# Macaron layer on one core: rope on even and odd tiles, one normalising op, and half of the output projection in the next sample's first slot

## What is computed

```
qkv = layernorm(x) @ Wqkv.T                      # 16 heads of 16 features
q = cos * q + rotate_half(q) * sin               # rotate_half: (x0, x1) -> (-x1, x0)
k = cos * k + rotate_half(k) * sin
scores = where(causal, q @ k.T / 4, -inf)
out = softmax(scores) @ v
x = x + out @ Wo.T
```

## Time and profile before

| | |
|---|---|
| median of 3 runs | 2371.58 us (2366.81 to 2373.09) |
| the profiled execution | 2371.06 us, its span 2369.3 us |
| instructions | 53760 |
| busy, share of the span | PE 90%, DVE 82%, ACT 57%, POOL 54% |
| granted TensorE clock, mean | 0.981 of full |
| attention stage, steady | 680 to 1840 us of the span, clock 1.00 |
| one steady sample | 45.57 us |

### The profile page before, as it was taken

The page is one execution under the profiler, slowest core; times in us unless marked ns, Lnnn a source line. Parts: engine busy times, 40 slices in busy tenths (PEclk is TensorE's granted clock), DMA queues, the critical chain, the costliest instruction groups (busy, mean ns, idle before and its releaser), DMA issues. The chain is left out here.

```text
span 2369.3 us, 53760 instructions
## 1 busy us (share of the span) xinstructions
PE 2140.1 (90%) x18188; PEld 1161.5 (49%) x18188; DVE 1946.5 (82%) x4345; ACT 1358.6 (57%) x2567; POOL 1283.0 (54%) x1459
## 2 busy tenths in 40 slices
PE   2999999489999999999999999999999986999999
PEld 1666666324444444444444444444444433666666
DVE  4777777469999999998999899899899865777776
ACT  2555545136666676666666666666666663455444
POOL 3666666335545554554555455455455425666664
PEclk9999999779999999999999999999999997999999
DMA  4566666333454444444445444444444513666664
GB/s 157 179 201 202 202 207 198 94 63 88 93 97 90 91 101 98 91 95 86 91 98 100 91 90 98 89 100 95 89 90 97 93 37 126 201 203 199 201 201 165
DMA packets 280353, 295.33 MB, mean 125 GB/s; under 512 B 45744, under 2 KB 263184, under 8 KB 280080
## 3 DMA queue, kind: packets, MB, share of 16 engines
q1 hardware_dynamic: 279536, 290.85, 48.8%
q10 hardware_dynamic: 544, 1.05, 0.1%
HBM read 140.08 MB, written 83.89 MB: 95 GB/s over the span
## 5 line engine op out<-in xcount | busy, mean ns | idle before, releaser
L820 ACT ACTIVATE at_probs<-at_st_ps 128x512 f32<-128x512 f32 x1280 | 748.2, 604 | 473.7 <-PE at_st_ps L925 466.8
L753 DVE TENSOR_REDUCE at_mx<-at_mx_ps 128x1 f32<-128x512 f32 (+3 forms) x1408 | 837.7, 633 | 125.9 <-PE at_mx_ps L907 124.7
L675 POOL TENSOR_SCALAR_AFFINE_SELECT at_probs<-at_probs 128x512 f32<-128x512 f32 x512 | 319.1, 635 | 677.9 <-ACT at_probs L820 673.9
L925 PE MATMUL at_st_ps<-at_q_stack,at_k_stack 49*128 49x512 f16 (+3 forms) x2048 | 459.8, 302 | 73.2 <-ACT at_probs L820 71.0
L902 PE MATMUL at_mx_ps<-at_k_stack,at_q_stack 48*128 48x512 f16 (+3 forms) x2048 | 494.1, 304 | 29.8 <-DVE at_mx L753 18.5
L431 ACT ACTIVATE f_h<-f_h_ps,f_b1s 128x512 f32<-128x512 f32 x256 | 175.9, 687 | 358.3 <-PE f_h_ps L473 347.2
L925 PEld LDWEIGHTS at_st_ps<-at_q_stack,at_k_stack 49*128 49x128 f16 x2048 | 135.9, 94 | 460.4 <-ACT at_probs L820 339.8
L907 PE MATMUL at_mx_ps<-mask,turn 64*128 64x128 bf16 (+2 forms) x1408 | 342.6, 244 | 0.0
L942 PE MATMUL at_pv_ps<-at_probs,at_v 128*32 128x512 f32 (+3 forms) x4096 | 329.8, 440 | 0.8 <-POOL at_probs L675 0.6
L489 PE MATMUL f_y_ps<-f_w2hi,f_hlo 128*128 128x256 f16 x1024 | 279.2, 273 | 0.0
L489 PE MATMUL f_y_ps<-f_w2lo,f_hhi 128*128 128x256 f16 x1024 | 279.2, 273 | 0.0
(11 more groups left out here) (117 smaller groups left out, 3921.9 us busy)
## 6 DMA issues: line engine op xcount, KB each, us to landing
at_q_stack<-qk_image SPq DMA_DIRECT2D x192, 128.0 KB, 4.5
at_k_stack<-qk_image SPq DMA_DIRECT2D x192, 128.0 KB, 4.8
f_x<-in_x SPq DMA_DIRECT2D x32, 512.0 KB, 5.6
f_w1hi<-w_hi SPq DMA_DIRECT2D x128, 128.0 KB, 2.4
f_w1lo<-w_lo SPq DMA_DIRECT2D x128, 128.0 KB, 2.1
f_b2s<-in_b SPq DMA_DIRECT2D x128, 128.0 KB, 3.8
f_w2hi<-w_hi SPq DMA_DIRECT2D x128, 128.0 KB, 4.2
f_w2lo<-w_lo SPq DMA_DIRECT2D x128, 128.0 KB, 4.3
```

Source lines behind the costliest of these rows:

```text
L675: nc.gpsimd.affine_select(out=ap, in_=ap, compare_op=ALU.is_ge, fill=0.0, base=0, pattern=[[0, d] for d in dims] + [[1, P]], channel_multi ...
L753: nc.vector.tensor_reduce(o_ap, i_ap, AX_X, ALU.max).then_inc(max_done, 1)
L820: nc.scalar.activation(probs[:, c, :], st_ps[c % 2][:], ACT.Exp, scale=DH ** -0.5).then_inc(exp_done, 1)
L925: ins = nc.tensor.matmul(bank[:, col:col + T - q0], k_stack[ss.par][rows, j + ha, kt * P:(kt + 1) * P], q_stack[ss.par][rows, j + ha, q0:T ...
```

## The change

1. **Rope.** The host permutes the columns of Wqkv for Q and K, so that a pair of tiles (t = 0 and 1 of Q, 2 and 3 of K) holds the even features of all heads and the odd ones. Rope is then even * cos - odd * sin and odd * cos + even * sin, between two tiles, without a swap of partitions. DVE only multiplies by the cosines. ACT gets a new op, `rope_raw`, which copies the projected tile from PSUM to the SBUF tile `raw` for POOL, once DVE's product is done. POOL makes the two products with the sines first (`rope_sin`), then the two sums (`rope_sums`), after the masks of the slot.
2. **Halves later.** In slots 1 and 2, ACT's high halves go from steps 0 and 2 to 3 and 5, DVE's low halves from steps 0 and 3 to 4 and 7. The products with the cosines stand at steps 3 and 6 of slot 0 and 2 and 6 of slot 1, the copies at steps 4 and 7 and 3 and 7.
3. **One normalising op.** The four multiplications of 4 x 16 columns become one of 4 x 4 x 16.
4. **Output projection.** Its tiles 2 and 3 move from step 10 of slot 3 to step 0 of the next sample's slot 0. `project_qk`'s first tile there moves to steps 1 and 2, and the second residual to step 2.
5. The rows of the DRAM image are read back with another pattern, to match the new order of features. Number and size of the DMAs stay.

```diff
@@ -526,7 +526,7 @@
...
         xT = Split(sb("xThi", [P, NC, T], F16), sb("xTlo", [P, NC, T], F16))
-        swapped = [sb(f"swapped{i}", [P, T], F32) for i in range(2)]
+        raw = [sb(f"raw{i}", [P, T], F32) for i in range(2)]
         by_cos = [sb(f"by_cos{i}", [P, T], F32) for i in range(2)]
@@ -555,6 +555,7 @@
...
         xT_lo, qk_done, rope_in, sin_done = sem("xT_lo"), sem("qk_done"), sem("rope_in"), sem("sin_done")
+        cos_done = sem("cos_done")
         rope_done, qk_hi, qk_lo, v_done = sem("rope_done"), sem("qk_hi"), sem("qk_lo"), sem("v_done")
@@ -604,7 +605,7 @@
...
                     for at, lo in enumerate(rows):
-                        img = image[2 * part + lo].rearrange("(j a r) n -> a r j n", a=2, r=DH)[par]
+                        img = image[2 * part + lo].rearrange("(r j a) n -> a r j n", a=2, r=DH)[par]
                         sp.dma_start(stack[HP * par + DH * at:HP * par + DH * at + DH, :, :], img).then_inc(
@@ -675,14 +676,19 @@
...
 
-            def rope(n, t):
+            def rope_sin(n, t):
                 idx = 4 * n.b + t
                 pool.wait_ge(rope_in, idx + 1)
-                nc.gpsimd.tensor_tensor(by_sin[t % 2][:], swapped[t % 2][:], sin_t[:], ALU.mult).then_inc(sin_done, 1)
-
-                wait(pool, qk_lo, idx - 1)
-                pool.wait_ge(sin_done, idx + 1)
-                nc.gpsimd.tensor_tensor(rotated[t % 2][:], by_cos[t % 2][:], by_sin[t % 2][:], ALU.add).then_inc(rope_done, 1)
+
+                wait(pool, rope_done, 4 * n.b + t // 2 * 2)
+                nc.gpsimd.tensor_tensor(by_sin[t % 2][:], raw[t % 2][:], sin_t[:], ALU.mult).then_inc(sin_done, 1)
+
+            def rope_sums(n, u):
+                pool.wait_ge(sin_done, 4 * n.b + 2 * u + 2)
+                for e, op in ((0, ALU.subtract), (1, ALU.add)):
+
+                    wait(pool, qk_lo, 4 * n.b + 2 * u - 1 + e)
+                    nc.gpsimd.tensor_tensor(rotated[e][:], by_cos[e][:], by_sin[1 - e][:], op).then_inc(rope_done, 1)
 
@@ -692,7 +698,8 @@
...
                 if g < 2 and sample(s + 1):
-                    rope(s + 1, 2 * g)
+                    rope_sin(s + 1, 2 * g)
+                    rope_sin(s + 1, 2 * g + 1)
                 if g == 2 and sample(s + 2):
@@ -711,7 +718,7 @@
...
                 if g < 2 and sample(s + 1):
-                    rope(s + 1, 2 * g + 1)
+                    rope_sums(s + 1, g)
             schedule(pool, slot)
@@ -724,8 +731,7 @@
...
                 wait(dve, rope_done, idx - 1)
-                nc.vector.tensor_tensor(by_cos[t % 2][:], x_ps[t % 2][:], cos_t[:], ALU.mult)
-                nc.vector.stream_shuffle(swapped[t % 2][:], x_ps[t % 2][:], [i ^ 1 for i in range(32)]).then_inc(rope_in, 1)
+                nc.vector.tensor_tensor(by_cos[t % 2][:], x_ps[t % 2][:], cos_t[:], ALU.mult).then_inc(cos_done, 1)
 
@@ -766,12 +772,10 @@
...
                 dve.wait_ge(inverse_done, G - 2)
-                for i in range(NT):
-                    ins = nc.vector.tensor_tensor(
-                        on[os.par][:, i, :].rearrange("p (j q d) -> p j q d", q=2, d=DH)[:, j:j + GH, half, :],
-                        turned[:, i, :, 0:DH],
-                        inverse[:, GH * i:GH * i + GH].rearrange("p (a d) -> p a d", d=1).broadcast_to([P, GH, DH]), ALU.mult)
-                ins.then_inc(on_done, 1)
+                nc.vector.tensor_tensor(
+                    on[os.par][:].rearrange("p i (j q d) -> p i j q d", q=2, d=DH)[:, :, j:j + GH, half, :],
+                    turned[:, :, :, 0:DH],
+                    inverse[:].rearrange("p (i a d) -> p i a d", i=NT, d=1).broadcast_to([P, NT, GH, DH]), ALU.mult).then_inc(on_done, 1)
 
@@ -782,11 +786,11 @@
...
                         maxima(s, g, n)
-                    if g in (1, 2) and sample(s + 1) and n in (0, 3):
-                        rope_low(s + 1, 2 * (g - 1) + (n == 3))
+                    if g in (1, 2) and sample(s + 1) and n in (4, 7):
+                        rope_low(s + 1, 2 * (g - 1) + (n == 7))
                     if group(G - 3) and n == 5:
                         normalise_output(s, g)
-                    if g < 2 and sample(s + 1) and n in (2, 6):
+                    if g < 2 and sample(s + 1) and n in (3 - g, 6):
                         begin_rope(s + 1, 2 * g + (n == 6))
@@ -799,7 +803,7 @@
...
                         add_residual(s + -1, 0)
-                    if g == 0 and sample(s + -2) and n == 0:
+                    if g == 0 and sample(s + -2) and n == 2:
                         add_residual(s + -2, 1)
@@ -825,6 +829,13 @@
...
 
+            def rope_raw(n, t):
+                idx = 4 * n.b + t
+                act.wait_ge(cos_done, idx + 1)
+
+                wait(act, sin_done, idx - 1)
+                nc.scalar.activation(raw[t % 2][:], x_ps[t % 2][:], ACT.Copy).then_inc(rope_in, 1)
+
             act.wait_ge(consts_set, 2)
@@ -836,8 +847,10 @@
...
                         exps(G, [n])
-                    if g in (1, 2) and sample(s + 1) and n in (0, 2):
-                        rope_high(s + 1, 2 * (g - 1) + (n == 2))
+                    if g in (1, 2) and sample(s + 1) and n in (3, 5):
+                        rope_high(s + 1, 2 * (g - 1) + (n == 5))
+                    if g < 2 and sample(s + 1) and n in (4 - g, 7):
+                        rope_raw(s + 1, 2 * g + (n == 7))
                     if group(G - 1) and n == 1:
@@ -1035,8 +1048,13 @@
...
                         turn_output(s, g)
-                    if g < 2 and sample(s + 1) and n in (0, 1, 4, 5):
-                        project_qk(s + 1, 2 * g + (n > 3), half=(n in (1, 5)))
+                    if g == 0 and sample(s + -2) and n == 0:
+                        project_o(s + -2, 2)
+                        project_o(s + -2, 3)
+                    if g == 0 and sample(s + 1) and n in (1, 2, 4, 5):
+                        project_qk(s + 1, int(n > 3), half=(n in (2, 5)))
+                    if g == 1 and sample(s + 1) and n in (0, 1, 4, 5):
+                        project_qk(s + 1, 2 + (n > 3), half=(n in (1, 5)))
                     if g == 2 and sample(s + 1) and n in (0, 1, 4, 5):
@@ -1045,9 +1063,9 @@
...
                         transpose_o(s + -1, s)
-                    if g == 3 and sample(s + -1) and n >= 9:
-                        project_o(s + -1, 2 * (n - 9))
-                        project_o(s + -1, 2 * (n - 9) + 1)
+                    if g == 3 and sample(s + -1) and n == 9:
+                        project_o(s + -1, 0)
+                        project_o(s + -1, 1)
 
@@ -1084,11 +1102,12 @@
...
     freqs = np.exp(np.float32(-np.log(10000.0)) * np.arange(0, DH, 2, dtype=np.float32) / np.float32(DH)).astype(np.float32)
-    angles = np.arange(T, dtype=np.float32)[None, :] * freqs[(np.arange(P) % DH) // 2][:, None]
-    sign = np.where(np.arange(P) % 2 == 0, -1.0, 1.0).astype(np.float32)[:, None]
+    angles = np.arange(T, dtype=np.float32)[None, :] * freqs[np.arange(P) // H][:, None]
+    halves = np.arange(D).reshape(H, DH // 2, 2).transpose(2, 1, 0).reshape(-1)
+    columns = np.concatenate([halves, D + halves, 2 * D + np.arange(D)])
     ins = {
         "x": L0_attn_x,
-        "WqkvT": np.asarray(L0_attn_Wqkv).T,
+        "WqkvT": np.asarray(L0_attn_Wqkv).T[:, columns],
         "WoT": np.asarray(L0_attn_Wo).T,
@@ -1097,7 +1116,7 @@
...
         "cos": np.cos(angles).astype(np.float32),
-        "sin": (np.sin(angles) * sign).astype(np.float32),
+        "sin": np.sin(angles).astype(np.float32),
     }
```

## The result

| | before | changed |
|---|---|---|
| median of the runs made side by side | 2372.34 us (2366.81 to 2381.37, 4 runs) | 2416.67 us (2411.64 to 2418.62, 4 runs) |
| ratio, 95% interval | | 1.0177 (1.0154 to 1.0200) |
| profiled execution, its span | 2371.06, 2369.3 us | 2411.64, 2409.9 us |

The change made the kernel slower by 1.8%, 44 us, where the forecast was +21 and the range ended at 2408. Direction right, size wrong by a factor of two.

The account below looks back on a forecast made before the run. The prediction took TensorE's own order to set the pace mostly, DVE close behind. Its terms, -0.09 + 0.3 + 0.17 + 0.28 = +0.66 us a sample over 31 samples, plus 0.5 for the prologue, gave 2392 us; range 2356 to 2408.

Parts of the forecast that it names:

- ScalarE in slot 1: Slot 1: added copies make the output's turn 0.91 us late, 0.74 won back from DVE; net +0.17 a sample.
- The move is worth nothing by itself and waits for the k stack: Slots 3 and 0: moving twelve matmuls gives -0.09 us a sample; waiting for the k stack adds +0.3.
- DVE as the limit at the end of slot 1: End of slot 1 into the next slot: TensorE held by DVE for 0.62 + 0.12 us a sample.
- Slot 0's raw copies at nothing: Slot 0: raw copies after the fifth and eighth exps were priced at nothing.
- Rival 1: Whole sample: DVE was the limit, ScalarE has room; 2345 us, or 2247 if all 4.0 us came through; chance together 0.18.
- Wait here 0.26 ... I take +0.3: Start of slot 0: TensorE's first maxima wait for the k stack's last DMA; +0.3 us a sample, ends 0 and 1.0.
- slot 2, "+0.28": Slot 2: output's turn some 0.2 us late, seventh exp and the ninth step 0.28 later; +0.28 a sample.
- rival 3: Slot 1's eighth step: low half against GpSimd's product makes DVE late by up to 1.0 us; 2423 us, chance 0.12.

Follow-up runs that it names:

- f1_best: Changed kernel with all output projection back at slot 3's end, copy o32 ahead of high half and raw copy, layernorm statistics a step later; 2380.45 us, ratio 1.0023.
- e4_o32_first: Changed kernel with ScalarE's copy o32 ahead of the high half and raw copy in their common step; 2400.32 us, 1.0105 of the kernel before.
- b2_norm_only: Kernel before with only the four normalising multiplications made one; 2365.57 us, ratio 0.9969.
- e1_proj_back: Changed kernel with the output projection all at the end of slot 3 again; 2400.50 us, 1.0110 of the kernel before.
- e2_old_read: Changed kernel with the old pattern of reading the DRAM image, so scores differ from the reference; 2403.30 us, 1.0124 of the kernel before.
- e3_stats_later: Changed kernel with slot 2's layernorm statistics one step later on VectorE; 2415.48 us, 1.0184 of the kernel before.
- f3_low_earlier: As f1_best, but slot 2's second high half and its low half each a step earlier; 2364.96 us, 0.9966 of the kernel before.
- f4_stats_split: As f3_low_earlier, with slot 2's layernorm statistics split: bn_stats behind the second step, small pair ops behind the third; 2347.17 us, 0.9881 of the kernel before.
- b3_halves_only: Kernel before with only the later places of the high and low halves in slots 1 and 2; 2399.97 us, ratio 1.0101.
- b1_proj_only: Kernel before with only the moved output projection, the product with the cosines a step later to match; 2390.67 us, ratio 1.0076.
- b4_new_read: Kernel before with only the new read pattern of the stacks, so scores differ from the reference; 2376.79 us, ratio 1.0011.

## Why the prediction was right in direction and wrong in size

**Right.** *ScalarE in slot 1.* The turn late by about 0.9, most of it covered by the 0.74 won from DVE: +0.17 forecast, +0.14 measured. f1_best shows both parts of that sum, 0.84 back and 0.70 below before; o32 ahead alone gives 0.45 back (e4_o32_first). *The move is worth nothing by itself and waits for the k stack.* *DVE as the limit at the end of slot 1:* b2_norm_only. *Slot 0's raw copies at nothing:* 10.46 in e1_proj_back. Rival 1 is out as the change stands. Yet work taken from DVE did pay 0.70 in slot 1, as soon as ScalarE's part of it stood behind the copy that TensorE waits for (f1_best); the one normalising op alone is 0.20 of that (b2_norm_only). The Trainium skill (Perfetto Trace Analysis, section Optimizing Scalar/DVE Operations), which the prediction cites, says that offloading to Scalar may make sense when DVE is saturated; the trace agrees there, for that slot and that order.

**Wrong, first step: "Wait here 0.26 ... I take +0.3" for the k stack.** Measured: 0.50 + 0.09 = 0.59, the 0.60 of waiting read above. The prediction took the stack's landing from the earlier trace rows as if the issues stayed, and item 5 changes just these DMAs. Six issues at 0.60 instead of 0.43 bring the last landing 0.34 to 0.39 us later; e2_old_read takes 0.36 of the 0.59 away and leaves 0.22 of waiting, so the term was about right for the old reads. The end of the range for this term, 1.0, held it. An access pattern that changes had no price in my list at all.

**Wrong, second step: slot 2, "+0.28".** It was worked out from ScalarE's order alone: the turn 0.2 late, the seventh exp 0.28 later. Neither holds the slot, since with o32 in time it stays as it is (e4_o32_first, f1_best). What does is DVE. The prediction moved DVE's low halves without asking what they leave and what they meet. They left the front of the slot, where DVE without them has time (0.53 of waiting in e3_stats_later), for its back, where it has none, and on the way two meetings with GpSimd arose: L103 with the sums (1.07 for 0.17), the low half with the masks (1.17 for 0.67). That this lock can decide was rival 3; I looked for it in slot 1's eighth step only, where GpSimd's product came out second. Taking the low half off the masks (f3_low_earlier, -0.48) and filling DVE's gap with the statistics (f4_stats_split, -0.53) gives back the 0.79 and more. The two wrong steps, some 0.3 and 0.5 above their terms, are the whole miss of 0.75 a sample.

**Where the 44 us are**, by the runs: 0.50 a sample for the moved projection (e1_proj_back), 0.84 for the halves' places (b3_halves_only), and 46.98 - 45.57 - 0.50 - 0.84 = 0.07 for the rest, rope without the shuffle and the one normalising op together. f4_stats_split, which keeps both, is 45.57 - 44.70 = 0.87 below the kernel before, so the order of the work around them took what they can give. How much of the 0.87 is the split of the statistics isn't shown; it wasn't tried in the kernel before. How much of b3's loss in slot 1 is the late copy and how much the low halves' new places wasn't separated. This takes the parts to add up; b1_proj_only, whose 0.63 isn't e1_proj_back's 0.50, shows that they do so only roughly.

## What to carry to other kernels

When an op moves on an in-order engine, list what the engine was waiting for at the old place and at the new one, and which op of the engine that shares its port runs beside each; a total per engine shows neither. Price every DMA whose access pattern changes, even at equal size and count. When one slot doesn't answer to an edit, look at what fills the gap that the edit left: e3_stats_later removed 0.9 us of waiting and won nothing, and the same ops in two pieces were worth 0.53 a sample.

## What the runs showed of the hardware

- The issue of a DMA on SP took 0.431 us when its 16 partitions lie one row apart in DRAM (and the eight rows of each partition 32 apart), and 0.598 when 16 rows apart (and the eight rows two apart), in both kernels, with the same 128 KB (e2_old_read, b4_new_read). Which of the two distances costs it wasn't separated.
- GpSimd's masks, which have one SBUF input, exclude a DVE op with two SBUF inputs just as its sums do: the two masks took 1.68 us beside the low half and 0.64 each alone. The Trainium skill (SBUF — State Buffer, section Who interferes with whom) has the exclusive lock; the trace agrees, and shows that a short op isn't spared: L103, of 4 columns, waited 0.90 us, and the low halves of the earlier trace rows, of 512, up to 1.04.
- DVE's L99, which reads one SBUF input, wasn't held by the sums beside it, nor they by it: in the changed kernel's slot 2 its four took 1.39 us, and the two sums 2.52, twice the shortest of the earlier trace rows.
- With the issues further apart, the last of the six DMAs landed sooner after its own issue: 0.70 us later at the issue was 0.34 to 0.39 at the landing (e2_old_read, b4_new_read).
